# One-pass integer up projection with token scales behind it, integers kept on chip, feed-forward steps of sixteen like slots

## What is computed

```python
def act_quant(x):
    scale = 127.0 / jnp.clip(jnp.max(jnp.abs(x), axis=-1, keepdims=True), 1e-05)
    return jnp.clip(jnp.round(x * scale), -128, 127) / scale

def weight_quant(w):
    scale = 1.0 / jnp.clip(jnp.mean(jnp.abs(w)), 1e-05)
    return jnp.clip(jnp.round(w * scale), -1, 1) / scale

h = bit_linear(x, w1)                    # act_quant(x) @ weight_quant(w1).T, 512 -> 2048
h = depthwise_conv1d(h, conv_w, conv_b)  # three taps along the 512 tokens
h = jax.nn.silu(h)
return bit_linear(h, w2)                 # act_quant(h) @ weight_quant(w2).T, 2048 -> 512
```

## Time and profile before

| | us |
|---|---|
| median of 3 runs | 1745.68 |
| lowest and highest | 1744.78, 1759.41 |
| profiled execution, its own time | 1753.9 |
| span in its profile (first to last instruction) | 1752.4 |
| busy: PE, PEld, DVE, ACT, POOL | 1550.8, 1218.5, 1060.4, 791.9, 622.9 |

### The profile page before, as it was taken

The page is one execution under the profiler, slowest core; times in us unless marked ns, Lnnn a source line. Parts: engine busy times, 40 slices in busy tenths (PEclk is TensorE's granted clock), DMA queues, the critical chain, the costliest instruction groups (busy, mean ns, idle before and its releaser), DMA issues. The chain is left out here.

```text
span 1752.4 us, 24975 instructions
## 1 busy us (share of the span) xinstructions
PE 1550.8 (88%) x8934; PEld 1218.5 (70%) x8956; DVE 1060.4 (61%) x1763; ACT 791.9 (45%) x1412; POOL 622.9 (36%) x584
## 2 busy tenths in 40 slices
PE   6599999999889999889999999567877789999997
PEld 5478878888668888767788888445556666666673
DVE  3468878788455553422233333269975877877775
ACT  2155555555321211113333444246666666766763
POOL 0134444444314666242412000265523443334440
PEclk9799999999899999999999999867678899999999
DMA  3123444333349999625533333598743112211202
GB/s 135 54 90 134 151 145 151 123 137 136 103 156 375 345 337 360 253 86 172 174 108 108 108 108 108 165 328 270 254 142 106 48 49 72 73 50 47 74 23 97
DMA packets 121334, 260.90 MB, mean 149 GB/s; under 512 B 15843, under 2 KB 24035, under 8 KB 119320
## 3 DMA queue, kind: packets, MB, share of 16 engines
q1 hardware_dynamic: 86440, 155.54, 26.6%
q0 software_dynamic: 17056, 67.12, 10.4%
q10 hardware_dynamic: 17744, 36.97, 5.6%
HBM read 147.13 MB, written 110.36 MB: 147 GB/s over the span
## 5 line engine op out<-in xcount | busy, mean ns | idle before, releaser
L2145 PE MATMUL f_banks<-xdT,w1q 128*128 128x512 f32 x992 | 239.6, 400 | 8.0 <-DVE b_h L2052 8.0
L2145 PEld LDWEIGHTS f_banks<-xdT,w1q 128*128 128x128 f32 x992 | 188.9, 192 | 49.4 <-DVE b_h L2052 9.1
L1978 POOL TENSOR_TENSOR b_h<-b_h,b_srow 128x512 f32<-128x512 f32 x112 | 143.4, 1327 | 205.5 <-ACT b_srow L2002 205.5
L202 PE MATMUL e_u_ps<-e_xs,w_shared 128*128 128x512 f32 x768 | 177.7, 392 | 6.1 <-DVE e_sg L1181 6.0
L202 PEld LDWEIGHTS e_u_ps<-e_xs,w_shared 128*128 128x128 f32 x768 | 145.0, 189 | 36.5 <-DVE e_sg L1181 6.1
L2009 ACT ACTIVATE b_h<-f_banks,cb,cw 128x512 f32<-128x512 f32 x128 | 104.6, 818 | 97.0 <-PE f_banks L2145 95.7
L2049 DVE SCALAR_TENSOR_TENSOR b_h<-f_banks,cw,b_h 128x511 f32<-128x511 f32 x128 | 95.7, 748 | 78.2 <-ACT b_h L2009 78.0
L1344 PE MATMUL e_u_ps<-e_w,e_xs 128*128 128x512 f32 x528 | 133.3, 401 | 2.0 <-DVE e_xs L1273 1.2
L1344 PEld LDWEIGHTS e_u_ps<-e_w,e_xs 128*128 128x128 f32 x528 | 95.9, 188 | 23.1 <-DVE e_xs L1273 1.6
L1281 DVE TENSOR_TENSOR e_hT<-e_r_ps,e_hT 128x256 fp32r<-128x256 f32 x69 | 29.2, 424 | 130.6 <-ACT e_hT L1121 130.6
L2123 PE MATMUL b_o_ps<-w2q,b_h 128*128 128x512 bf16 x441 | 102.9, 388 | 2.8 <-ACT b_h L1993 1.5
(11 more groups left out here) (236 smaller groups left out, 3152.8 us busy)
## 6 DMA issues: line engine op xcount, KB each, us to landing
e_xe<-slots_in_scratch SPq DMA_DIRECT2D x69, 256.0 KB, 2.6
experts_out_scratch<-e_ye ACTq DMA_DIRECT2D x69, 256.0 KB, 2.0
xin<-in_x SPq DMA_DIRECT2D x16, 512.0 KB, 4.4
xres<-in_x SPq DMA_DIRECT2D x16, 512.0 KB, 5.3
x_scratch<-x SPq DMA_DIRECT2D x32, 256.0 KB, 2.0
xn_scratch<-xn SPq DMA_DIRECT2D x32, 256.0 KB, 2.0
xn2T_scratch<-x2T SPq DMA_DIRECT2D x16, 512.0 KB, 4.4
e_x<-x_scratch SPq DMA_DIRECT2D x32, 256.0 KB, 5.4
```

Of the source, the lines that this page charges most:

```text
L202: mm = pe.matmul(n.u_ps[:, (2 * q + j) % 4], n.w_shared[q // n.KH][:, pa, at:at + P], xs[:, pb, k], start=(k == 0 and (pa, pb) == PASSES[0 ...
L1978: pool.tensor_tensor(ht, ht, srow[:], ALU.mult).then_inc(u_done, 1)
L2145: mm = pe.matmul(f_ps[:, u % RING], w1q[:, k, m * P:(m + 1) * P], xdT[:, part, k], start=(k == 0 and part == 0), stop=(k == KD - 1 and par ...
```

## The change

The rounded integers of x go straight from `xq` through PE into `xqT` in bf16, all 8 batches kept on chip. `dequantise`, the scratch tensor xdT_d, its stores and loads, the high and low parts and `first_parts` are gone. The up projection multiplies integers by w1q (bf16 too) in 4 matmuls instead of 8. Its result lacks the token's scale; since the taps mix neighbouring tokens, the scale has to be applied before them. A new SBUF ring `u` of 6 tiles takes the scaled tiles: for 6 of 16 tiles DVE multiplies the PSUM bank by the scale row `xrow` into u; for the other 10 ACT copies the bank to u and POOL multiplies there. The taps read u. PE and ACT make `xrow` each step as they do srow. Each step has one unit of work a slot: `down` is cut in quarters, POOL's products and ACT's lifts are spread by two dictionaries. The sums over w2q move into `fuse`, to its steps 6 and 7.

In the excerpt, `v` counts tiles over all steps.

```diff
-        n.w1q = keep("w1q", [P, KD, DH], FR)
+        n.w1q = keep("w1q", [P, KD, DH], BF16)
+        n.xqT = keep("xqT", [P, B, KD, S], BF16)
@@ fuse, POOL, SP, ACT, DVE, PE
             def run(s, back, mid, front, par):
+                if s == B - 2:
+                    weight_sum(0)
+                    weight_sum(1)
                 if loads(s):
...
-                if j == 0 and not (isinstance(b, int) and b == 0):
-                    act.wait_ge(xd_out, b * 16)
                 act.wait_ge(dT_full, b * TB + j + 1)
-                act.activation(xdT_out[:, :, j * P:(j + 1) * P], d_ps[:, j % 2], ACT.Copy).then_inc(dT_copied, 1)
+                act.activation(dst, d_ps[:, j % 2], ACT.Copy, bias=-OFFSET).then_inc(dT_copied, 1)
...
-                        if back:
-                            dequantise(s, j)
...
-                    mm = pe.transpose(d_ps[:, j % 2, k], xd[:, j, k * P:(k + 1) * P], ident[:])
+                    mm = pe.matmul(d_ps[:, j % 2, k], low_half[:, par, j, k * P:(k + 1) * P, 0], ident_h[:], start=True, stop=True)
@@ ffn
+    UB = 6
+    AHEAD = 3
+    BY_VECTOR = (1, 4, 7, 9, 12, 15)
+    BY_POOL = tuple(m for m in range(KF) if m not in BY_VECTOR)
@@ POOL
-                if quant and f1:
-                    pool.wait_ge(row_done, s)
+            def token_scale(v):
+                if v < B * KF and v % KF in BY_POOL:
+                    if v % KF == BY_POOL[0]:
+                        pool.wait_ge(xrow_done, v // KF + 1)
+                    pool.wait_ge(evicted, count(v, BY_POOL))
+                    pool.tensor_tensor(u[:, v % UB], u[:, v % UB], xrow[:, v // KF % 2], ALU.mult).then_inc(scaled_pool, 1)
...
+                if f1:
                     for m in range(KF):
+                        token_scale(s * KF + m + AHEAD)
+                        if quant:
+                            for k in products.get(m, ()):
+                                product(s - 1, k)
@@ ACT
                     for m in range(KF):
-                        act.wait_ge(f_full, s * KF + m + 1)
-                        act.activation(tile(s, m), f_ps[:, (s * KF + m) % RING], ACT.Identity, bias=cb[:, m:m + 1],
+                        v = s * KF + m
+                        evict(v + AHEAD)
+                        wait_scaled(act, v)
+                        act.activation(tile(s, m), u[:, v % UB], ACT.Identity, bias=cb[:, m:m + 1],
                                        scale=cw[:, m, 1:2]).then_inc(mid_tap, 1)
+                        if m == 0 and s >= 2:
+                            lift_tile(s - 2, KF - 1)
                         if m >= 1:
                             silu(m - 1)
-                        if quant and m == 2:
-                            scale_row()
+                        if m == 3:
+                            if quant:
+                                scale_row()
+                            if front:
+                                token_row()
@@ DVE
+                    dve.tensor_tensor(u[:, v % UB], f_ps[:, v % RING], xrow[:, v // KF % 2], ALU.mult).then_inc(scaled_dve, 1)
...
-                    f, ht = f_ps[:, u % RING], tile(s, m)
+                    f, ht = u[:, v % UB], tile(s, m)
...
+                        token_scale(s * KF + m + AHEAD - 1)
                         taps(m)
+                        if quant and m == 0:
+                            token_scales()
@@ PE
-                        for part in range(2):
-                            mm = pe.matmul(f_ps[:, u % RING], w1q[:, k, m * P:(m + 1) * P], xdT[:, part, k],
-                                           start=(k == 0 and part == 0), stop=(k == KD - 1 and part == 1))
+                        mm = pe.matmul(f_ps[:, v % RING], w1q[:, k, m * P:(m + 1) * P], n.xqT[:, s, k],
+                                       start=(k == 0), stop=(k == KD - 1))
...
+                        if f2:
+                            down(m // 4, m % 4)
+                        if quant and m == 2:
+                            max_transposes()
+                        if m == 3:
+                            if quant:
+                                scale_row()
+                            if front:
+                                token_row()
```

More of the change, by code:

```diff
@@ L1569, in run @@
                         load_ctx(s + 2, par)
-                if not isinstance(s, int) or s >= 2:
-                    store(s - 2)
-                if isinstance(s, int) and s == B:
-                    store(s - 1)
             for b in range(2):
@@ L1625, in _ @@
             pool.memset(eps[:], EPS_LN)
+            pool.tensor_copy(ident_h[:], ident[:]).then_inc(identh_done, 1)
+            pool.memset(n.lift[:], -OFFSET)
             gather(0, 0)
@@ L1792, in run @@
                     aggregate(1, mv2_done, s * 2 * TB + (2 * TB if front else TB))
-                elif back:
-                    for j in range(TB):
-                        dequantise(s, j)
             whole(dve, run)
@@ L1983, in _, with evict @@
         def _(act):
+            def evict(v):
+                if v < B * KF and v % KF in BY_POOL:
+                    act.wait_ge(f_full, v + 1)
+                    if v >= UB:
+                        act.wait_ge(conv_done, v + 1 - UB)
+                    act.activation(u[:, v % UB], f_ps[:, v % RING], ACT.Copy).then_inc(evicted, 1)
             def run(s, f1, quant, f2, front):
@@ L2094, in run @@
                         dve.tensor_tensor(ht, ht, srow[:], ALU.mult).then_inc(u_done, 1)
-                        if m in (3, 7):
-                            outputs(2 + m // 4)
-                if f1:
-                    if front:
-                        low(0)
-                    half_max(1)
-                    if front:
-                        for k in range(1, KD):
-                            low(k)
-                if f2 and not quant:
-                    outputs(2)
-                    outputs(3)
+                        if m == 3:
+                            outputs(s - 2, 2)
+                elif f2:
+                    for j in range(TB):
+                        outputs(s - 2, j)
+            for v in range(AHEAD - 1):
+                token_scale(v)
             whole(run)(dve)
@@ L2156, in max_transposes, with row, token_row @@
                     mm.then_inc(amt_full, 1)
+                def row(acc, columns, done):
+                    for j in range(TB):
+                        mm = pe.matmul(acc[:, j], columns[:, j:j + 1].to_broadcast([P, P]), ident[:], start=True, stop=True)
+                    mm.then_inc(done, 1)
                 def scale_row():
                     pe.wait_ge(scale_steps, s * 4)
-                    for j in range(TB):
-                        mm = pe.matmul(q_ps[:, 0, j], s2[:, j:j + 1].to_broadcast([P, P]), ident[:], start=True, stop=True)
-                    mm.then_inc(row_full, 1)
+                    row(q_ps[:, 0], s2, row_full)
+                def token_row():
+                    if s == 0:
+                        pe.wait_ge(xrow_done, 1)
+                    row(q_ps[:, 1], n.dqa[:, (s + 1) * TB:(s + 2) * TB], xrow_full)
                 if f2 and not quant:
```

278 lines of the change are left out of this document (134 added, 144 removed).

## The result

The changed kernel takes 1912.73 us (median of 4 runs, 1904.8 to 1916.89) where the kernel before takes 1748.59 in the same session: 1.0922 times as long, 95% interval 1.0858 to 1.0987. The profiled execution has a span of 1913.7 us, 161.3 more than before. The prediction was 1846, range 1755 to 1890: slower was right, the size was 67 us short, and the time is outside the range.

What follows compares the result with a forecast made beforehand. PE and a loop through DVE were taken to set the step together. Fuse -10, head of ffn +4, step 0 +5, steps 1 to 7 +99, last steps +2: together +100 on 1745.7, so 1846 us, range 1755 to 1890.

Steps and rivals of the forecast that it cites:

- the port: Feed-forward steps: DVE's taps with two SBUF inputs and POOL's instructions exclude each other; step 62.5 us, between 59 and 67.
- Rival B: Feed-forward: taps and POOL don't block each other, steps of 54 us, no stall in fuse's step 6; 1761 us; chance 0.13.
- PE stops being the bound: Feed-forward step: PE's matmuls, transposes and two scale rows sum to about 32 us, against a step of 49.85.
- the walk: One feed-forward step followed instruction by instruction from maximum to maximum: 52.4 us with nothing in the way, against 49.85.
- the chain at the head of a step: Step's start: transposes, up tiles, copies, taps, token scales and rows come before POOL's first product, 15.8 us after H.
- H: The moment the preceding feed-forward step's last maximum ends, from which the forecast times one step.
- the clock's 1.6: Head of a feed-forward step: PE idles about 9 us, its clock drops to 0.50, adding 1.6 us a step.
- the head and step 0: Start of ffn: token row, copy and POOL scale before the first tap, +4; ten POOL scales in DVE's way, +5.
- The term for the sums: Fuse's step 6: POOL's two big sums stand beside DVE's combining of the experts' outputs, +10 us.
- The term for `dequantise`: Fuse: four `dequantise` leave DVE's 20 us step, 1.6 us in each of 6 steps, -9 us.
- The last steps: End of fuse: ACT's 9.77 us wait for a store and the slow dequantise beside first_parts both go, -11 us.
- rival C: Feed-forward: PE's clock stays at 1.2 GHz, so steps take 70 us; 1888 us; chance 0.03.

Runs made afterwards that it cites:

- experiments 1 and 6: 6: changed kernel with ACT's copy of tile m+3 behind middle tap m, 1839.31 us; also with POOL's multiplications replaced by memsets, 1764.95. For 1 see experiment 1.
- experiment 5: experiment 1 with DVE's outputs in slots 2, 6, 10 and 14, 1802.29 us; also with filler matmuls and token scales ahead of the first taps, 1783.26 us.
- experiment 7: Changed kernel with each of POOL's 26 multiplications a step by a row made a multiplication by 1.0, one SBUF input instead of two: 1849.48 us.
- experiment 1: Changed kernel with each of POOL's 26 multiplications a step replaced by two memsets of the same tile, which read nothing: 1827.07 us.

## Why the prediction was wrong in size and right in sign

**Right: the port.** The prediction took two SBUF inputs beside POOL's reads as mutually exclusive, from one instruction of the experts stage, and priced it at 62.5 - 52.4 = 10.1 us a step. It measures 10.3 and 10.4 (experiments 1 and 6), of which 1 to 2 may be POOL's shorter work there. Its shape too: taps at 1.2 to 1.27 us, POOL's products at 1.66, both within what was named. It chose the middle of two ends (6.6 and 14.6), since POOL's side was poorly known; the products do pay, 0.34 us each. The trace shows the block itself as strict as the far end took it, every held tap ending 0.55 us after a POOL instruction, while the price came out in the middle. So that the price agrees within 0.3 us is partly luck. Rival B is refuted.

**Wrong: "PE stops being the bound", so it was left out of the walk behind slot 5.** A sum of 32 us of work was taken as a reason that PE is never waited for. But PE's list is in order, and a down group in it waits for DVE's outputs through two banks. The trace of before couldn't show this wait, since a step's down group stood elsewhere and in one piece; the code did: `pe.wait_ge(o_done, w - 1)` and the slots 4, 8 and 12. PE waited 17.2 us a step there. From POOL's first product to the last maximum the prediction has 62.5 - 4.4 - 15.8 = 42.3 us, measured are 46.0: 3.7 that stood in no term. Taking the wait away gives 4.2 where the port is gone (36.8 to 32.6, experiment 5), and then the walk is right for this part: 52.4 - 4.4 - 15.8 = 32.2.

**Too short: the chain at the head of a step.** POOL's first product was forecast for H+15.8, or H+17.4 with the clock's 1.6; it started at H+21.2, outside the 15 to 19 that were named. PE was idle 8.6 us ahead of the transposes (9 forecast), and these took 1.97. But the clock stayed at 0.50 to H+12.4, so that the two rows behind were through at H+12.7 and not at H+8.5, and up tile 5, for which ACT's copy ahead of middle tap 2 stands, came at H+15.7 and not at H+11.4. This makes the other 3.8 us: 71.7 is 7.7 more than the forecast step of 64. The walk had the copies ahead of the middle taps in it and took them as given; that this order costs 10 us a step, most of it here, it didn't see.

Over seven steps, of which the first and the last are shorter (67.1 and 68.7), the two make the difference between +99 and +147, 48 of the 67 us by which the sum fell short. The remaining 19 are fuse (11), the end (2) and 6 that lie in no stage: the profiled execution of the kernel before was 8.2 us above its median, that of the changed kernel 2.5 above its own.

**The rest of ffn** was near: +9 for the head and step 0 as forecast (+11 if PE's first row is counted to it), +4 for +2 at the end. The parts are near too. From PE's first row to the end of step 0's last maximum the changed kernel takes 47.8 us and experiment 1 43.4, so the port makes 4.5 (forecast 5), and the head 6.4 (forecast 4).

**Fuse: -10 forecast, +1 measured.** The term for the sums, +10, measures +11.5 by the four combines: right. The term for `dequantise`, -9 over six steps at 1.5, measures 1.1 a step, -6.6, if all that the five steps lost is put down to it. The last steps, -11, measure -8.5 (step 7 and what follows): ACT no longer waits for a store, but the quantisation starts 2.0 us after the last aggregate, and PE's waits and clock stay. And the first step of fuse took 4.7 us more, at a clock of 0.50 where it was 0.69; no step of the prediction speaks of it. It isn't bound to the change: in experiment 7, whose fuse is that of the changed kernel, and in both runs with POOL's token scales of tiles 0 to 2, this step took 27.2 to 27.6 us at a clock of 0.67 to 0.69, and in all other runs of the changed fuse 30.0 to 32.0 at 0.50 to 0.53. Why the clock differs stays open.

**The range** was built on cases that share one walk, so an error in the walk moved all of them: rival C alone, with its 70 us a step, came near, but its clock of 0.50 throughout did not (0.76 in a step). Two independent costs need two independent ends.

## What to carry to other kernels

When a change makes an engine light, look in its list for waits on small rings: here PE's waits for two banks were worth about 4 us a step, in an engine that a sum of work had cleared. Put work that runs ahead (a copy for tile m+3) behind the work that is due (the middle tap of tile m), above all on an engine whose list is in order; here one moved line was worth 73 us, most of it where a step begins. And before moving an operand from PSUM to SBUF, ask what the instruction's other input is and what POOL reads meanwhile: here it cost 10 us of a 70 us step.
